# Four attention layers on one core: the loads of the start are re-dealt to the queues, the constants' products ahead of the first layer are dropped, and all engines' lists are replaced

## The reference

```python
def reference(x, ctx_2048, ...):
    x = _L0_xattn_ref(x, ctx_2048, ...)      # 8 heads over the 64 channels; norm over the whole sequence
    x = _L1_xattn_ref(x, ctx_2048, ...)      # 16 heads, keys and values from the normed context, tanh(gate) on the result
    x = _L2_xattn_ref(ctx_2048, x, ...)      # queries from x; keys and values from context and x (128 keys); rmsnorm, gelu MLP
    x = _L3_xattn_ref(x, ctx_2048, ...)      # self-attention, cross-attention, gelu MLP, a layernorm ahead of each
    return x

# in each of the layers
scores = einsum(q, k) * scale                # masked
probs  = softmax(scores)
out    = einsum(probs, v) @ Wo + bo          # added to the residual
```

## Time and profile before

| what | value |
|---|---|
| median of 3 runs | 1220.33 us (1220.17 to 1222.36) |
| the profiled execution: time, span of its instructions | 1221.77 us, 1220.0 us |
| PE busy | 1189.9 us (98%) |
| VectorE busy | 958.0 us (79%) |
| ScalarE busy | 848.0 us (70%) |
| GpSimd busy | 614.0 us (50%) |
| HBM traffic over the span | 23.53 MB read, 2.10 MB written |

### The profile page before, as it was taken

The page is one execution under the profiler, slowest core; times in us unless marked ns, Lnnn a source line. Parts: engine busy times, 40 slices in busy tenths (PEclk is TensorE's granted clock), DMA queues, the critical chain, the costliest instruction groups (busy, mean ns, idle before and its releaser), DMA issues.

```text
span 1220.0 us, 35295 instructions
## 1 busy us (share of the span) xinstructions
PE 1189.9 (98%) x13174; PEld 974.5 (80%) x13174; DVE 958.0 (79%) x2298; ACT 848.0 (70%) x2275; POOL 614.0 (50%) x1003
## 2 busy tenths in 40 slices
PE   8999999999999999999999999999999999999998
PEld 7778787787887878788787887878787787877877
DVE  3778886969788797787969788697887969789764
ACT  2877676787867668686776667677686777866543
POOL 2653663637455473644646456373654645363341
PEclk7999999999999999999999999999999999999999
DMA  6501000000000000010100100000000000000000
GB/s 207 192 3 28 2 27 2 16 20 25 15 6 12 22 14 12 12 30 1 29 15 2 32 2 20 17 16 2 25 12 17 24 8 16 2 12 2 2 6 10
DMA packets 27623, 27.91 MB, mean 23 GB/s; under 512 B 11072, under 2 KB 25408, under 8 KB 26816
## 3 DMA queue, kind: packets, MB, share of 16 engines
q1 hardware_dynamic: 25808, 23.42, 6.3%
q10 hardware_dynamic: 1648, 2.23, 0.6%
HBM read 23.53 MB, written 2.10 MB: 21 GB/s over the span
## 4 chain that ended last, share of the span: by engine, by line
PE 75%; DVE 11%; issue 4%; POOL 4%; ACT 4%; DMA 1%; SPq 0%; POOLq 0%; DVEq 0%; ACTq 0%
PE bank L932 9%; PE bank L659 9%; PE bank L942 8%; PE bank L539 7%; PE attended L614 7%; PE bank L599 7%; PE bank L665 5%; PE bank L694 4%; PE bank L720 4%; PE bank L683 3%; PE bank L707 3%; PE bank L652 2%; PE bank L510 2%; ACT p_a L575 2%; DVE nmax_a L554 2%
## 5 line engine op out<-in xcount | busy, mean ns | idle before, releaser
L586 POOL TENSOR_SCALAR p_a<-p_a,rec_a 128x256 f32<-128x256 f32 x512 | 248.6, 502 | 116.3 <-DVE rec_a L560 116.3
L575 ACT ACTIVATE p_a<-bank,nmax_a 128x256 f32<-128x256 f32 x512 | 237.9, 475 | 57.3 <-DVE nmax_a L554 55.8
L554 DVE TENSOR_REDUCE nmax_a<-bank 128x2 f32<-128x512 f32 x256 | 170.7, 680 | 25.7 <-PE bank L539 25.3
L599 PE MATMUL bank<-ident,p_a 128*128 128x128 f32 x1024 | 143.7, 275 | 2.6 <-POOL p_a L586 1.4
L539 PE MATMUL bank<-cc,q_a 64*128 64x256 f32 x1024 | 133.9, 392 | 1.5 <-DVE p_a L632 0.3
L599 PEld LDWEIGHTS bank<-ident,p_a 128*128 128x128 f32 x1024 | 115.8, 141 | 19.6 <-issue 11.8
L614 PE MATMUL attended<-p_a,v_a 128*64 128x256 f32 x1024 | 125.2, 386 | 0.1
L539 PEld LDWEIGHTS bank<-cc,q_a 64*128 64x128 f32 x1024 | 93.6, 186 | 32.4 <-issue 19.4
L575 ACT ACTIVATION_READ_ACCUMULATOR p_a<-bank,nmax_a 128x1 f32 x512 | 105.1, 205 | 0.0
L614 PEld LDWEIGHTS attended<-p_a,v_a 128*64 128x64 f32 x1024 | 67.0, 136 | 44.0 <-issue 12.0
L632 DVE COPY p_a<-bank 128x512 f32<-128x512 f32 x128 | 86.4, 680 | 8.0 <-PE bank L599 7.9
(11 more groups left out here) (265 smaller groups left out, 2890.6 us busy)
## 6 DMA issues: line engine op xcount, KB each, us to landing
xx<-in_x SPq DMA_DIRECT2D x32, 128.0 KB, 2.8
cc<-in_ctx SPq DMA_DIRECT2D x32, 128.0 KB, 2.9
wc<-in_wc SPq DMA_DIRECT2D x3, 1024.0 KB, 11.5
k_c<-in_ctx SPq DMA_DIRECT2D x16, 128.0 KB
res_a<-in_x SPq DMA_DIRECT2D x16, 128.0 KB, 2.3
wb<-in_wb SPq DMA_DIRECT2D x2, 1024.0 KB, 6.2
out<-y_out SPq DMA_DIRECT2D x16, 128.0 KB, 2.2
wb<-in_wb ACTq DMA_DIRECT2D x2, 512.0 KB, 6.6
```

The costliest lines, as they stand in the source:

```text
L554: dve.tensor_reduce(nmax_a[:, n, e, :], ps[:, :].rearrange("p (q k) -> p q k", q=KT), AX.X, ALU.max, negate=True).then_inc(A.s["max"], 1)
L575: last = act.activation(p_a[:, j % 2, n, e, qt, :], ps[:, qt * D:(qt + 1) * D], ACT.Exp, bias=nmax_a[:, n, e, qt:qt + 1], accum_out=sum_a[ ...
L586: last = pool.tensor_scalar(p_a[:, j % 2, n, e, qt, :], p_a[:, j % 2, n, e, qt, :], rec_a[:, n, e, qt:qt + 1], 1.0, ALU.mult, ALU.mult)
L599: last = nc.tensor.transpose(ps[:, kt * D + qt * P:kt * D + (qt + 1) * P], p_a[:, j % 2, n, e, qt, kt * P:(kt + 1) * P], ident[:, :])
```

## The change

Three things are edited.

- `WARM_UP` goes from 13 to 0, and `IDLE_WORK` from 62 to 63. The 13 letters `w` at the front of PE's string are gone.
- The loads of kv0 and kv1 of wb and of kv1 of wc move from ScalarE's queue to SP's, as three steps of their own behind cols and bv_raw. In SP's new string the first of them follows bv_raw directly; then come the masks of the first pair, kv1 of wb, the context cc, kv1 of wc, q0 and o0, the bias rows, and then the second pair's x, which waits for L510; w1, w2 and qkvo0 follow behind that.
- The strings of all five engines and `BANK` are replaced from end to end. Apart from the constants and the three new steps on SP, each string has the same letters as before, in another order.

```diff
--- before.py
+++ after.py
@@ -60,8 +60,8 @@
 UNITS = H0
 BANKS = 7
 AHEAD = 4
-WARM_UP = 13
-IDLE_WORK = 62
+WARM_UP = 0
+IDLE_WORK = 63
 SHIFTED_APART = 13
...
 ORDER = {
     "sp": (
-        "nksnssdksnsebssnfsndnkebbndfnknfnedenybbbkfndnkydenkebdnfbnyffdnnyebyeknkbednfnynkkdbddnefenyfnkyyfbnedfnykbkn"
-        "enbfykebdnenbdefkynffydyyy"),
+        "nkssebsnsssnsnksdfkssdennsdnbbkdefndnnnebynkfnfybkbedenbkfdydnnfkdeyenbfnyknfdnbkynenefnddfykebknybbnnfeekfbny"
+        "fneybdnndkbnfdyneekdbfyfkyyyy"),
     "pe": (
-        "wwwwwwwwwwwwwsnksssknnkqqanakkskdaanddkdddaadddsdnsddaddddaqddqaadkdddkkddnanaddbkbdndbdddaaddbdbddbaabkeddnee"
...
+        "sknsnksqqnanakkksaadskddkdnddadnsddsdaddaaddddqddqaaddkdkdkddnanabddkbddbdddnaaddbdbddbaanbddekeedededdddddqqa"
...
@@ -1312,9 +1312,6 @@
                 nc.scalar.dma_start(dst, src).then_inc(setup["wqk_in"], 16)
             for dst, src in ((wv_raw[:, :, :], dram["wv0"]), (wo_raw[:, :, :], dram["wo0"])):
                 nc.scalar.dma_start(dst, src).then_inc(setup["wvo_in"], 16)
-            load_weights(nc.scalar, wb, "kv0", "b_kv0")
-            load_weights(nc.scalar, wb, "kv1", "b_kv1")
-            load_weights(nc.scalar, wc, "kv1", "c_kv1")
             yield
             nc.scalar.wait_ge(setup["rows_in"], 64)
             nc.scalar.activation(tanh_gate[:, :], gate[:, :], ACT.Tanh).then_inc(setup["tanh"], 1)
@@ -1362,6 +1359,12 @@
             yield
             for dst, src in ((cols[:, :], dram["cols"]), (bv_raw[:, :], dram["bv0"])):
                 sp.dma_start(dst, src).then_inc(setup["cols_in"], 16)
+            yield
+            load_weights(sp, wb, "kv0", "b_kv0")
+            yield
+            load_weights(sp, wb, "kv1", "b_kv1")
+            yield
+            load_weights(sp, wc, "kv1", "c_kv1")
             yield
             load_weights(sp, wb, "q0", "b_q0")
             load_weights(sp, wb, "o0", "b_o0")
```

More of the change, by code:

```diff
@@ L115 @@
[L115 to L119, removed]
@@ new lines @@
+        "dkhchkbcnccdbddcaabkdhbdhdcedcddaacedddecdeeddqqdfdddfddfbeeebeanefnfefkkfkaaagkdggkggbhkdhkcdhbccdcbddcaabdhd"
+        "cdhcdkbcddecaadefedfdfdeedddddffddfkdkwbkefkebeekbehkehhgbbgbgbgegeeewwweckccckhcweeehewwwwecwecwwwcwwgcgggfgf"
+        "wwwfcwwwccwwwwwfccfwwwfkfcwwcwwwwcwhchwwfwwwfwwfhhhffwwwfwwwwfwwwwwwwwwwhwwwhhhh"),
+    "act": (
+        "skkqqqqnsaakaandaadaakaddaaaaddaqaaqqqaaddkaaknkaabnadbdadbabdabbabaaaekdadaedqqdqeaeaebeeenqaaendbaagdbggbkaa"
+        "bbdabcaedaaccaaccdcdceaaqqqfddqeaeeaebeennfefffabfadkkkagakgdgahhbacbhbkcdbabdaacacecacacaddafeddqeeqqqebeeenf"
+        "aafenffafdakbkakgadggaadhaacbbkbbdhbhaccakccecdaacadaefddqeqqeebqeneefaefffafnakakkbdgaakhggadahchkbbbbcabdada"
+        "caceaaccacaddqefddqeeeeqbeeaqfenfnfafbaagfakkakgghdakadchkhbbcabbaddcbaccaedcaadcaafddeeeqqeebeeaqfnefafbqfaaf"
+        "dkkkaagknaggahhbbchbdbcaabkddcceaaccacadadafddeeeeqeqeenfqfnqeffaafbkkbkaagaadkdaggabhkhchbcabdadbbcaacdccecad"
+        "aeaafqdqdeqeqaeeeebnnfafeffafbakkkgaadgkgdahadbbacdbachbhaabcdckcceaadcaafddeqeeeeeeqnfqfqnebfffaakbkkaagaakdg"
+        "gaahdhbcbbkcbhbdadacceaaccaacddaafddeeqeeeqeefqnfqffenfaakkkbagadaabggbahakbhbdchbckaddbaccaaeccdacaadeafddqee"
+        "eeqeeqbqfnanfeaffafabkkkgdggakahkcabbdacbbhhaabcdaccadecaacdadafeddqeqeqeeqbeenafafenbfffakkadgaagkgadahcbkbbh"
+        "chbaacdkdccbaacaecaaddafdedeqeqeeeeqfbfnefafbafqnaadgakagkgkaahkbcbbhdhckbabadcacadeccaacddaaeqqfddqeqebeeeebn"
+        "feffnfafakkkaagaagdgkaahkbcdbbhcbhaacdcbcdcacaeaafdadafdfdfffekekkbeeebeeehkbbgbbgbgeckheheceeeeececcccgggfcff"
+        "cfffccccchkfhhfffffhhh"),
@@ L186 @@
-    "2351042351042351604253")
+    "01234560125346012536454014503623613463450215064210365426452160345215641620356142504365204365120463546513426025"
+    "61561053260415326043215643251643250160413602451346143641560234154356315643015423560142106120614325061342534502"
+    "34650243162501260260412360241534651346153016530165021320143526430562341056236243621360432510432561045324563210"
+    "43562431032135421563402142051240265314021645365140635124035123463260153462016421650413625041632504321504163025"
@@ L189, in fill_places @@
+    "45302164156213546210435213201435261045312046532046531053416052346105304651320413240132640132645012364502136502"
+    "4163524163502416350216")
 def fill_places():
```

110 lines of the change are left out of this document (48 added, 62 removed).

## The result

The changed kernel takes 1199.81 us (median of 4 runs, 1199.37 to 1201.1) against 1220.88 of the kernel before beside it; the ratio is 0.9828, with a 95% interval of 0.9811 to 0.9845. That is 21 us faster; forecast were 1218.0, with 1214.2 to 1222.0 as the range. The profiled execution has a span of 1198.0 us, 22.0 less than before.

The account below looks back on a forecast made before the run. TensorE was taken as the bound, with 17.6 us of gaps all an order can win. Start 1.3 plus body 1.0 took 2.3 us off span 1220.0, giving 1217.7 and median 1218.0 us, range 1214.2 to 1222.0.

Parts of the forecast that it names:

- The change: the body: 40 to 1140 us: new orders close one gap near 925 us, gain 1.0 us; no sign for the rest.
- all stretches as the best: Bound for the body: every stretch has gaps like the best one, 7 us in all, 10.6 less.
- better-body rival: Body comes out one deviation better, 2.8 us more gain, 1215.2 us in all; chance 0.22.
- Constants: Start: removing the 13 warm-up products costs nothing, as PE waits beside them; L1268 starts at about 5.3 us.
- L599 at 29.58: Start: first attention transpose begins at 29.58 us instead of 30.90, 1.32 us earlier, with 5.66 us at the lower clock.
- the case priced at 2.8 us more: Start: if the clock rose at once with L510's wide products, another 2.8 us would be gained.
- The warning to warm up first: Start: the skill's advice to run matmuls first, read as against the change; removal would cost up to 0.8 us.
- qkvo0: Late 1 MB weight load, issued near 27 us, landing at worst at 38.5; nothing booked, bound 0.5 us.
- Start in sum: Start of the kernel: all its changes together booked as a gain of 1.3 us.
- Stage c: Near 925 us: the longest gap, 1.35 us ahead of L683, closes; 1.0 us gained in stretch 840 to 940.
- The end: Last 80 us: same steps in nearly the same list, so zero gain, between -1 and +1 us.
- Slower by x1's transposes: Body: L652 of x1 waits for VectorE's L640, 0.8 us in each of ten pairs, 1226.0 us; chance 0.13.

Follow-up runs that it names:

- lone stream: TensorE's instructions of either kernel run without other engines, waiting only for its own earlier product in the same bank: 1158.4 us before, 1155.0 after.
- the last experiment: Both kernels' lists with banks rechosen from reader finish times in their own traces, second longest free: 1219.69 us with old lists, 1199.73 with new.

## Why the prediction was wrong

The direction and most of the start were right; the body was not. The step that failed is **"The change: the body"**, with the sentence of the first part on which it rests, that 17.6 us of gaps are all that an order can win. It failed twice.

- *The bound.* PE's busy time was read as work. The lone stream has 1158.4 us of it, not 1189.9, and in the body the old lists lost 34.5 us between passes 674 and 12000, not some 17. In its place held a better measure in the same row: the weight loads and the passes of a stretch. The Trainium skill says it outright in "Perfetto Trace Analysis", section "Identifying the Most-Contended Engine": a tensor engine's headroom is to be judged by the busy share of its weight loads (or the flops reached). This trace agrees, with 1.7% more for the loads and 0.7% for PE's busy time where the passes rose by 1.8%. The prediction did not weigh that rule. The share has to be set against the lone stream and not against 100%: alone the loads are busy for 83.2% (831.89 of 1000 us), in the body for 80.3% before and 81.6% after. What is missing, 3.5% and 1.9% of 83.2, is some 38 and 20 us of the 1100 (an estimate), near the 34.5 and 19.8 of the table.
- *The size.* The body's lists were taken as a random new deal, "no sign", with a deviation of 2.8 us. They are worth 18.2 us without the new start (some 1.8 of it at the end, by the table of passes), beyond even the end called "all stretches as the best" (10.6). The sign that the better-body rival names, more PE work between many dependent steps, was given 2.8 us and 0.22; it pointed the right way. That this slack in PE's list is the reason is not shown, and at the line that gained most the traces speak against it. Of the 5.7 us that the old list lost at L599, only 0.4 lay at the 23 of 256 groups with less than 8 us (timed in the lone stream) between their scores and their transposes; the other waits stood at groups with more, up to 33 us. So what the other engines had to do first seems to count there, which no run changed alone. Shown is that order and not banks or start made the waits shorter, at many lines.

Point by point:

- *Constants* (booked as free): right in the sum, 1221.24 without and 1221.44 with them. L1268 came at 6.51 instead of 5.3, since wk landed later. That L1276 started at 9.14 (forecast 9.1) is luck in part: xx came at 6.08 and not at 7.03, the copy of wT then waited 0.80 us for L1268, and TensorE 0.70 us for k_c at L652.
- *L510 at 14.9*: right, 14.63 for the first pass and 15.05 for the others.
- *L599 at 29.58*: it was 27.52. The step took over 5.66 us of lower clock behind the first wide product. L433 at 17.78 has the full rate (1.21 us for its eight passes, against 2.08 in the earlier trace rows), 3.15 us behind L510's first pass. So the lower level ended at least 2.5 us sooner behind the first wide product, which at half the rate is worth 1.3 us or more (an estimate). That is the way of the case priced at 2.8 us more; 2.1 came in all, and no row splits the rest.
- *The warning to warm up first*: neither kernel lost by leaving the constants out, before (1221.24 and 1221.44) or after (1199.81 and 1199.86). With the constants in front the rate was full at L1268, and the clock stood at 0.50 from 10 to 23 us. Put in front of the kernel after, they brought L599 to 26.71 instead of 27.52 in the profiled execution, as much as the 0.8 us that the prediction gave them; in the median time this doesn't show. The advice that the prediction names, from the Trainium skill ("TensorE: Matmul & The Clock Gate", section "Why this matters for your kernels"), stands there for timing matmuls accurately; the prediction widened it to a warning against the change.
- *qkvo0*: the wait came, 1.29 us against a bound of 0.5, so the bound was wrong; without the wait the time was the same (1199.77).
- *Start in sum* (1.3): 2.5 us with the old body.
- *Stage c* (1.0): the gap near 925 closed, as forecast; the scores there start as close to the product before as in the lone stream.
- *The end* (0, within 1): 1.8 us, by the table of passes.
- *Slower by x1's transposes*: did not come. Who waited for L640 in the kernel after (us, times), where before it was 0.3:

```profile
  PE attended L1235: 0.4, 1
  PEld bank L652: 0.2, 1
```

## What to carry to other kernels

Measure how full TensorE is by what it gets done in a stretch (weight loads, passes), and find the floor by running its list alone. Idle time of a row that stands in the lone run too is no wait for others. The distance to that floor, here 59 us and still 40 now, is the most that an order of the lists can win (waits that no order removes are in it), and the gaps in its busy time are only a part of it. When all lists are replaced at once, splice old and new at a place where the same steps are done and the same banks are held; two splices tell where a gain lies. A table of buffers must follow the times at which readers finish; here another choice among the buffers free in time cost nothing.

## What was not expected of the hardware

- Two quite different orders of 13,150 passes take TensorE alone the same time: 1158.4 and 1155.0 us, 3.4 of it for the constants (one run of each).
- The choice among seven PSUM banks weighs heavily: banks chosen without the readers' times cost about 298 us with the old lists and 362 with the new. The clock, at 0.97 on the mean from 40 to 1140 us with the old lists, has a share in it.
- The stretch of half clock at the start has another length from run to run in the kernels with constants in front. In the 19 runs of the kernel before beside the second set, times of 1221.0 to 1222.0 go with a mean granted clock of 0.994, 1220.0 to 1220.9 with 0.996, and one of 1217.9 with 0.997; in the set beside the last experiment the two overlap (up to 1221.57 with 0.996). The kernel after has 1.000 in every run, while its L1268 runs at 270 ns a pass against 150 in the earlier trace rows: the column shows a granted 1.00 where the durations are those of the lower level. In the trace of the kernel after, the first entry of the clock is its rise, at 17.35 us.
